# Output matmuls of a decoder layer's second attention: from bursts of four steps in shared PSUM banks to one step at a time in a bank of their own

## The chip, the cores and the metric

The kernel runs on one core of a Trainium2 chip, as one program for the whole input. The metric is the device time of one execution in microseconds; the median of three runs of the kernel before is 2312.41 us.

## What is computed

The reference is one decoder layer over x of shape (8, 512, 256), with a context of shape (8, 1024, 128): a first attention (16 heads of 16, with a convolution and a position matmul ahead of it), a layer norm, a second attention, a layer norm, and a routed feed-forward part with two more norms. The change lies in the second attention alone:

```python
q, k, v = _heads(x @ Wq + bq), _heads(x @ Wk + bk), _heads(x @ Wv + bv)
att = jnp.einsum('bhqd,bhkd->bhqk', q, k) * scale
att = jnp.where(causal[None, None], att, -jnp.inf)
y = jnp.einsum('bhqk,bhkd->bhqd', jax.nn.softmax(att, axis=-1), v)
qc = _heads(x @ Wcq + bcq)
kc, vc = _heads(cross_input @ Wck + bck), _heads(cross_input @ Wcv + bcv)
attc = jnp.einsum('bhqd,bhkd->bhqk', qc, kc) * scale
y = y + jnp.einsum('bhqk,bhkd->bhqd', jax.nn.softmax(attc, axis=-1), vc)
```

So there is a causal self attention over 512 keys and a cross attention over 1024 keys, both in fp32, for 16 heads and 8 batches.

## The kernel before, in words

Every engine has its own instruction stream, written out in Python in the order in which it runs; engines wait for each other on semaphores. The batches follow one another; the routed feed-forward part of batch b - 1 is spread through batch b.

**The steps.** The second attention of a batch is made in 48 steps (`ALL_STEPS`): 16 self steps (4 groups of 4 heads, times 4 blocks of 128 keys) and 32 cross steps (4 groups, times 8 blocks). A step s has, for each of its 4 heads g:

- a transposed score (`scoresT`, L1533): keys on the partitions, up to 512 queries in the columns, a contraction of 32 rows; in self steps it has 512, 384, 256 or 128 columns, since queries ahead of the keys are left out. ScalarE makes its exponential (`probabilities`, L651, recorded at L659) into `pT` in `work`, which holds six steps (`PT_SLOTS`); for self steps GpSimd blanks the diagonal (`causal`, L529).
- outputs (`pv`, L1558, recorded at L1570): values times probabilities, a contraction over 128 rows into 32 columns, added up over four steps (`BURST`) in one PSUM bank. In the trace each fp32 matmul stands as two instructions, so the outputs of a step are 8 rows and a burst of four steps 32.

Softmax needs a row maximum ahead of the transposed scores. For it the plain scores (`scores`, L1513 and L1517) are made seven steps ahead (`LEAD`), and VectorE reduces them (`maxima`, L1030 and L1033). Five such groups of four are made in four self steps, so that scores and maxima are through after step 36. A transpose (`max_rows`, L1530) and an addition (`put_rows`, L1055) put the maxima into a spare row of the queries. After the last burst of a group of heads its outputs are transposed (`o_transpose`, L1582), and VectorE divides and adds (`finish`, L1063 to L1069).

**The order on TensorE.** In every step a score and a transposed score alternate, head by head, on different row groups. `burst_behind` lets a whole burst of outputs follow the last pair of every fourth step, up to burst 8; from step 38 on (`SINGLES_FROM`, `SINGLES_BEHIND`) outputs are made one step at a time, two steps behind, by `pv_step`.

**The banks.** PSUM has eight banks of 512 fp32 columns. Banks 0 to 3 are VectorE's ring: scores, outputs, max rows and transposed outputs take the next of four slots in an order that `slot_uses` writes out, and `free_slot` (L1207) lets TensorE wait until VectorE has read the use four before. Banks 4 to 7 are ScalarE's ring (`exp_bank`, L377): the n-th transposed score waits for the exponential of n - 4. From step 37 on (`LATE_STEP`) there are no more scores; then ScalarE has six banks and the rest two.

```python
RING, EXP_RING = 4, 4
LATE_BANKS, LATE_EXP_BANKS = (6, 7), (4, 5, 0, 1, 2, 3)
```

**The order on VectorE.** In step s: from step 37 on first a piece of the feed-forward part of the batch before (`third_sums` at 37, `third_norm` at 39, a convolution at 40, `last_sums` at 42, `last_norm` at 44), then the step's maxima, then the read-out of a finished burst (`outputs`, L1040) where `outputs_ready` names one, in four bursts behind two transposes of the next batch's queries and keys (L761), then `put_rows` and `finish`. The read-out of burst j stands at step 4 (j + 1) up to j = 8, and at 4 (j + 1) + 1 behind that.

Of the kernel before, what the change touches and what calls it, by code (L numbers as in the profile page):

```python
# [37 lines left out]
def decoder_layer(nc, x, xT, ctxT, conv_w, pe_w, qkT, vT, outT, Wk, bk, Wq, bq, Wv, bv, Wck, bck, Wcq, bcq,  # L38
# [12 lines left out]
    NT = S // P  # L51
# [27 lines left out]
    RING, EXP_RING = 4, 4  # L79
# [17 lines left out]
    USES = ALL_SCORES + (4 + BURSTS) * HG + FFN_USES  # L97
# [18 lines left out]
    with ctx:  # L116
# [147 lines left out]
        sT_mm, pT_ready, causal_done = sem("sT_mm"), sem("pT_ready"), sem("causal_done")  # L264
        rec_step, y_done = sem("rec_step"), sem("y_done")
# [63 lines left out]
        def burst_behind(s):  # L329

            return [s // BURST - 1] if s % BURST == 0 and s > 0 else []

        def outputs_ready(s):

            j = s // BURST - 1
            return [j] if s % BURST == (0 if j < SINGLES_FROM else SINGLES_BEHIND - 1) and j >= 0 else []

        def slot_uses(ffn):
# [13 lines left out]
            for s in range(ALL_STEPS):  # L352
# [3 lines left out]
                order.extend(("pv", j) for j in outputs_ready(s))  # L356
                order.extend(("rows",) + part for part in rows_behind(s))
                order.extend(("o",) + part for part in outputs_behind(s))
            order += [("pv", ALL_STEPS // BURST - 1), ("o", CROSS, HG - 1)]
# [16 lines left out]

        def exp_bank(n):  # L377
            return bank[:, RING + n % EXP_RING if n < FIRST_LATE else LATE_EXP_BANKS[(n - FIRST_LATE) % len(LATE_EXP_BANKS)], :]

        def last_exp(at):  # L380

            return max(n for n in range(FIRST_LATE, ALL_SCORES) if LATE_EXP_BANKS[(n - FIRST_LATE) % len(LATE_EXP_BANKS)] == at)
# [173 lines left out]
        def _(act):  # L556
# [37 lines left out]
            def batch(b, prev=True, ahead=True):  # L594
# [140 lines left out]
        def _(dve):  # L735
# [206 lines left out]
            def batch(b, prev=True, ahead=2):  # L942
# [97 lines left out]
                def outputs(j):  # L1040

                    use = uses["pv", j]
                    dve.wait_ge(slot_in, base + use + 1)
                    if j < HG or j % 2 == 0:
                        nc.vector.tensor_copy(o_rows[:, SELF if j < HG else CROSS, :], slot(uses, use)).then_inc(slot_out, 1)  # L1045
                    else:
                        dve.wait_ge(slot_out, base + uses["pv", j - 1] + 1)
                        nc.vector.tensor_tensor(o_rows[:, CROSS, :], slot(uses, use), o_rows[:, CROSS, :], ALU.add).then_inc(slot_out, 1)
# [148 lines left out]
        def _(pe):  # L1197
# [112 lines left out]
            def batch(b, prev=True, ahead=True):  # L1310
# [222 lines left out]
                def scoresT(s, g):  # L1533
# [8 lines left out]
                    if n >= FIRST_LATE + len(LATE_EXP_BANKS):  # L1542
# [170 lines left out]
```

## Time and profile before

| what | value |
|---|---|
| runs | 2309.06, 2312.41, 2316.03 us; median 2312.41 us |
| span of the profiled execution | 2303.2 us, 9.2 us under the median of the runs (its own time is not listed apart from theirs) |
| TensorE, weight loads | busy 2183.0 us (95%), 991.3 us (43%) |
| VectorE | 1869.5 us (81%) |
| ScalarE | 1384.6 us (60%) |
| GpSimd | 189.0 us (8%) |
| granted TensorE clock, mean | 0.970 |

The span runs from the first to the last instruction. Times in the rows below are in us from the span's start; most are of batch 3 (the fourth), whose second attention lies at 976 to 1133. TensorE's rows overlap, since matmuls on different row or column groups run side by side and their ends are modelled, so its busy share says little of how much work it had.

### The profile page before, as it was taken

The page shows a single profiled execution, that of the slowest core. Times are in us where ns is not written, and L with a number is a line of the kernel's source. Part 1 is how long each engine was busy: PE and PEld are TensorE (multiplying, and loading weights), DVE is VectorE, ACT ScalarE, POOL GpSimd, SP SyncE. Part 2 cuts the span into 40 slices and gives each one's busy share as a digit, 9 for nine tenths or more (in the row PEclk, how much of TensorE's full clock was granted, in tenths as well). Part 3 has the DMA queues.
Part 4 walks back from the last instruction along what each step waited for, and adds up shares of the span by engine and source line. Part 5 has one row for each costly group of instructions (what it writes and reads, how often), then busy time and mean ns, then how long its engine had stood idle before and what let it go on. Part 6 is the DMA issues. An engine that isn't in the chain of part 4 may idle for free.

```text
span 2303.2 us, 37677 instructions
## 1 busy us (share of the span) xinstructions
PE 2183.0 (95%) x13138; PEld 991.3 (43%) x13138; DVE 1869.5 (81%) x5137; ACT 1384.6 (60%) x2977; POOL 189.0 (8%) x349
## 2 busy tenths in 40 slices
PE   5999999999999999999999999999999999989992
PEld 2354434543345434554335543454334543345432
DVE  6858879788888879788797887978888787978854
ACT  2834687456854579446783467745686457844560
POOL 3011001100011000110001100010001100001000
PEclk7899999999999999999999999999999999999995
DMA  3600034000520006100160002500043000510000
GB/s 110 130 10 1 1 67 81 10 1 1 113 44 10 1 19 121 27 1 1 38 119 10 2 1 58 100 10 1 1 91 57 10 1 11 105 33 1 1 10 9
DMA packets 250845, 81.69 MB, mean 35 GB/s; under 512 B 236064, under 2 KB 247328, under 8 KB 250656
## 3 DMA queue, kind: packets, MB, share of 16 engines
q1 hardware_dynamic: 250656, 79.29, 16.8%
q8 instruction: 104, 1.70, 0.3%
q14 instruction: 85, 0.70, 0.1%
HBM read 16.35 MB, written 4.19 MB: 9 GB/s over the span
## 4 chain that ended last, share of the span: by engine, by line
PE 79%; DVE 10%; ACT 7%; issue 3%; DMA 0%; SPq 0%; POOL 0%; DVEq 0%; POOLq 0%; ACTq 0%
PE bank L1517 23%; PE bank L1570 13%; PE bank L1555 7%; PE bank L1204 7%; PE bank L1513 5%; ACT work L603 4%; PE bank L1552 4%; PE bank L1470 4%; DVE work L770 4%; PE bank L1333 3%; PE bank L1320 2%; PE bank L1356 2%; PE bank L1530 2%; PE bank L1582 1%; ACT k_c L636 1%
## 5 line engine op out<-in xcount | busy, mean ns | idle before, releaser
L659 ACT ACTIVATE work<-bank 128x512 f32<-128x512 f32 (+3 forms) x1536 | 739.7, 550 | 529.8 <-PE bank L1552 264.1
L1033 DVE TENSOR_REDUCE top_half<-bank 128x1 f32<-128x512 f32 x1024 | 625.5, 682 | 21.0 <-PE bank L1517 21.0
L1517 PE MATMUL bank<-k_c,q_c 32*128 32x512 f32 x2048 | 628.6, 634 | 0.0
L1555 PE MATMUL bank<-q_c,k_c 32*128 32x512 f32 x2048 | 526.2, 633 | 0.0
L603 ACT ACTIVATE work<-work,neg 128x512 bf16<-128x512 bf16 x512 | 362.6, 715 | 30.5 <-DVE work L770 29.8
L1517 PEld LDWEIGHTS bank<-k_c,q_c 32*128 32x128 f32 x2048 | 274.6, 184 | 245.1 <-DVE top_half L1033 159.8
L770 DVE TENSOR_SCALAR_CACHE_REDUCE work<-bank 128x512 bf16<-128x512 f32 x512 | 322.4, 686 | 43.7 <-PE bank L1302 33.6
L1570 PE MATMUL bank<-work,v_flat 128*32 128x512 f32 (+3 forms) x3072 | 321.8, 544 | 5.5 <-ACT work L659 5.0
L1030 DVE CUSTOM_DVE_ANT_0 masked<-bank,mask_w 128x384 bf16<-128x384 f32 (+3 forms) x512 | 223.8, 488 | 79.5 <-PE bank L1513 74.0
L1552 PE MATMUL bank<-q_s,k_s 32*128 32x512 f32 (+3 forms) x1024 | 258.1, 471 | 0.0
L1555 PEld LDWEIGHTS bank<-q_c,k_c 32*128 32x128 f32 x2048 | 218.4, 183 | 78.4 <-ACT work L659 48.6
L1513 PE MATMUL bank<-k_s,q_s 32*128 32x384 f32 (+3 forms) x1024 | 204.5, 482 | 3.8 <-DVE top_s L1030 3.6
L1570 PEld LDWEIGHTS bank<-work,v_flat 128*32 128x32 f32 x3072 | 86.6, 109 | 236.8 <-ACT work L659 119.0
L1320 PE MATMUL bank<-k,q 32*128 32x512 bf16 x448 | 140.5, 390 | 16.4 <-DVE work L770 14.3
L1552 PEld LDWEIGHTS bank<-q_s,k_s 32*128 32x128 f32 x1024 | 141.7, 185 | 22.0 <-ACT work L659 9.1
L1513 PEld LDWEIGHTS bank<-k_s,q_s 32*128 32x128 f32 x1024 | 104.5, 187 | 81.5 <-DVE top_s L1030 41.0
L1333 PE MATMUL bank<-work,v 128*32 128x512 bf16 x512 | 133.3, 386 | 0.8 <-DMA work<-work 0.5
L529 POOL TENSOR_SCALAR_AFFINE_SELECT work<-work 128x512 f32<-128x512 f32 x128 | 81.2, 634 | 606.4 <-ACT work L659 606.4
L518 POOL TENSOR_SCALAR ln_var<-mv 128x4 f32<-128x4 f32 x32 | 8.7, 272 | 1473.8 <-DVE mv L779 1473.8
L1356 PE MATMUL bank<-k,identb 128*128 128x512 bf16 x448 | 122.0, 391 | 5.8 <-DVE work L770 3.6
L963 DVE TENSOR_SCALAR work<-work,rden 128x512 bf16<-128x512 bf16 x424 | 123.0, 350 | 4.5
L1045 DVE COPY featA<-bank 128x512 f32<-128x512 f32 x64 | 44.3, 692 | 93.6 <-PE bank L1570 93.6
(194 smaller groups left out, 2214.1 us busy)
## 6 DMA issues: line engine op xcount, KB each, us to landing
xT_pad<-xT SPq DMA_DIRECT2D x16, 256.0 KB, 3.3
ctx_sb<-ctxT SPq DMA_DIRECT2D x8, 512.0 KB, 3.4
x_res<-x SPq DMA_DIRECT2D x8, 512.0 KB, 4.8
out<-r_sb SPq DMA_DIRECT2D x8, 512.0 KB, 3.1
work<-work SPq DMA_TRANSPOSE x112, 4.4
qk_sb<-qkT SPq DMA_DIRECT2D x1, 512.0 KB, 4.7
pe_sb<-pe_w SPq DMA_DIRECT2D x1, 256.0 KB, 4.0
v_sb<-vT SPq DMA_DIRECT2D x1, 256.0 KB, 5.4
```

The costliest lines, as they stand in the source:

```text
L603: nc.scalar.activation(e1[:, h % E1_SLOTS, t, :], s1[:, h % 2, t, :], ACT.Exp, bias=neg1[:, h % 2, t:t + 1], scale=-1.0, accum_out=den1[:, ...
L659: nc.scalar.activation(pT[:, s % PT_SLOTS, g, q0:S], exp_bank(n)[:, 0:S - q0], ACT.Exp, scale=SCALE).then_inc(pT_ready, 1)
L770: nc.vector.tensor_scalar(s1[:, h % 2, t, :], bank[:, (NT * h + t) % A1_BANKS, :], -SCALE, None, ALU.mult, ALU.min, accum_out=neg1[:, h % ...
L1030: nc.vector.tensor_tensor_reduce(masked[:, g, 0:n], scores[:, 0:n], mask_w[:, S - n:S], -1.0, -MASKED, ALU.add, ALU.min, top_s[:, i % 2, u ...
L1033: nc.vector.tensor_reduce(top_half[:, i % 2, g, u // 2, u % 2:u % 2 + 1], scores, AX.X, ALU.max, negate=True).then_inc(slot_out, 1)
L1320: mm(bank[:, n % A1_BANKS, :], q_1[rows, i, P * t:P * (t + 1)], k_1[rows, i, :], start=True, stop=True, tile_position=(GW * (h % GH), 0)). ...
L1333: last = mm(bank[GW * g:GW * (g + 1), PV1_BANKS[h // 8], :], v1[:, h, j, :], p1T[:, h % E1_SLOTS, :, j, :], start=(h % 2 == 0 and j == 0), ...
L1513: mm(dst[:, 0:n], q_s[rows, i, P * u:n], k_s[rows, i, 0:n], start=True, stop=True, tile_position=(GW * g, 0)).then_inc(slot_in, 1)
L1517: mm(dst, q_c[rows, i, P * t:P * (t + 1)], k_c[rows, i, S * half:S * (half + 1)], start=True, stop=True, tile_position=(GW * g, 0)).then_i ...
L1552: mm(dst[:, 0:S - q0], k_s[rows, i, q0:q0 + P], q_s[rows, i, q0:S], start=True, stop=True, tile_position=(GW * g, 0)).then_inc(sT_mm, 1)
L1555: mm(dst, k_c[rows, i, P * u:P * (u + 1)], q_c[rows, i, :], start=True, stop=True, tile_position=(GW * g, 0)).then_inc(sT_mm, 1)
L1570: last = mm(dst[GW * g:GW * (g + 1), q0:S], v_flat[:, at:at + GW], pT[:, s % PT_SLOTS, g, q0:S], start=(s % BURST == 0), stop=(s % BURST = ...
```

## The change

- Bank 7 (`PV_BANK`) becomes the outputs' own, with two semaphores of its own: `pv_mm` is raised by each step of outputs, `pv_out` by each read-out of a burst. The first step of a burst waits for the read-out of the burst before.
- Outputs are made one step at a time in all steps, two steps behind (`PV_BEHIND`), right behind the fourth transposed score of a step. `pv` and `burst_behind` are gone.
- ScalarE's ring has three banks (4, 5, 6) up to step 36; from step 37 on it has six in another order. VectorE's ring keeps its four banks (0 to 3), and after that one (6), and outputs take no slot in it.
- ScalarE waits for a free probability slot by the step (`pv_mm`) and no longer by the burst.
- The read-out of every burst j stands at step 4 (j + 1) + 1 of VectorE's order.

```diff
-    RING, EXP_RING = 4, 4
+    RING, EXP_RING, PV_BANK = 4, 3, 7
-    SINGLES_FROM, SINGLES_BEHIND = 9, 2
+    PV_BEHIND = 2
-    LATE_BANKS, LATE_EXP_BANKS = (6, 7), (4, 5, 0, 1, 2, 3)
+    LATE_BANKS, LATE_EXP_BANKS = (6,), (5, 4, 0, 1, 2, 3)
...
         def outputs_ready(s):
-            j = s // BURST - 1
-            return [j] if s % BURST == (0 if j < SINGLES_FROM else SINGLES_BEHIND - 1) and j >= 0 else []
+            return [s // BURST - 1] if s % BURST == PV_BEHIND - 1 and s >= BURST else []
...
+        def exp_at(n):
+            return RING + n % EXP_RING if n < FIRST_LATE else LATE_EXP_BANKS[(n - FIRST_LATE) % len(LATE_EXP_BANKS)]
+        def exp_before(n):
+            return max((i for i in range(n) if exp_at(i) == exp_at(n)), default=None)
...
                     if s >= PT_SLOTS:
-                        act.wait_ge(slot_in, base + uses["pv", (s - PT_SLOTS) // BURST] + 1)
+                        act.wait_ge(pv_mm, b * ALL_STEPS + s - PT_SLOTS + 1)
...
-                    dve.wait_ge(slot_in, base + use + 1)
+                    dve.wait_ge(pv_mm, b * ALL_STEPS + BURST * (j + 1))
...
-                    if n >= FIRST_LATE + len(LATE_EXP_BANKS):
-                        pe.wait_ge(pT_ready, b * ALL_SCORES + n - len(LATE_EXP_BANKS) + 1)
-                    elif n >= FIRST_LATE + 2:
+                    if exp_before(n) is not None:
+                        pe.wait_ge(pT_ready, b * ALL_SCORES + exp_before(n) + 1)
+                    elif n >= FIRST_LATE:
                         pe.wait_ge(slot_out, base + uses["late"])
-                    elif n >= EXP_RING:
-                        pe.wait_ge(pT_ready, b * ALL_SCORES + n - EXP_RING + 1)
...
                 def pv_step(s):
-                    pv(s // BURST, range(s % BURST, s % BURST + 1))
+                    kind, i, u = part_of(s)
+                    pe.wait_ge(pT_ready, b * ALL_SCORES + GH * (s + 1))
+                    if kind == SELF:
+                        pe.wait_ge(causal_done, b * SELF_STEPS + s + 1)
+                    if s % BURST == 0 and b * PV_BURSTS + s > 0:
+                        pe.wait_ge(pv_out, b * PV_BURSTS + s // BURST)
...
+                        last = mm(bank[GW * g:GW * (g + 1), PV_BANK, q0:S], v_flat[:, at:at + GW], pT[:, s % PT_SLOTS, g, q0:S],
+                                  start=(s % BURST == 0), stop=(s % BURST == BURST - 1), tile_position=(0, GW * g))
+                    last.then_inc(pv_mm, 1)
...
                         scoresT(s, g)
-                        if g == GH - 1 and s - SINGLES_BEHIND >= BURST * SINGLES_FROM:
-                            pv_step(s - SINGLES_BEHIND)
-                    for j in burst_behind(s):
-                        if j < SINGLES_FROM:
-                            pv(j)
+                        if g == GH - 1 and s >= PV_BEHIND:
+                            pv_step(s - PV_BEHIND)
```

On TensorE, in the cross steps of the first batch, around the end of step 20, before. L1517 is a score, L1555 a transposed score, L1570 outputs; `slot_out` is raised by VectorE, `pT_ready` by ScalarE's exponentials:

```order
L1517 MATMUL bank<-k_c,q_c 128x512 [waits slot_out]
L1555 MATMUL bank<-q_c,k_c 128x512 [waits pT_ready]
L1517 MATMUL bank<-k_c,q_c 128x512 [waits slot_out]
L1555 MATMUL bank<-q_c,k_c 128x512 [waits pT_ready]
L1570 MATMUL bank<-work,v_flat 32x512 [waits slot_out,pT_ready]
L1570 MATMUL bank<-work,v_flat 32x512 x15
L1517 MATMUL bank<-k_c,q_c 128x512 [waits slot_out,pj_evac]
L1555 MATMUL bank<-q_c,k_c 128x512 [waits pT_ready]
```

The same place now (the score is at L1519, outputs at L1569):

```order
L1569 MATMUL bank<-work,v_flat 32x512 [waits pv_out,pT_ready]
L1569 MATMUL bank<-work,v_flat 32x512 x3
L1519 MATMUL bank<-k_c,q_c 128x512 [waits slot_out]
L1555 MATMUL bank<-q_c,k_c 128x512 [waits pT_ready]
L1519 MATMUL bank<-k_c,q_c 128x512 [waits slot_out]
L1555 MATMUL bank<-q_c,k_c 128x512 [waits pT_ready]
L1519 MATMUL bank<-k_c,q_c 128x512 [waits slot_out]
L1555 MATMUL bank<-q_c,k_c 128x512 [waits pT_ready]
L1519 MATMUL bank<-k_c,q_c 128x512 [waits slot_out]
L1555 MATMUL bank<-q_c,k_c 128x512 [waits pT_ready]
L1569 MATMUL bank<-work,v_flat 32x512 [waits pT_ready]
L1569 MATMUL bank<-work,v_flat 32x512 x3
```

The sixteen output matmuls that stood together behind every fourth step now stand in fours behind the four pairs of each step.

On VectorE, at the change from step 36 to step 37 of a batch that carries the feed-forward part, before (L1045 is the read-out of burst 8, L775 to L929 are `third_sums`, L1055 is `put_rows` of step 38):

```order
L1045 COPY featA<-bank 128x512 [waits slot_in]
L775 BN_STATS stats<-xs 128x6 x4
L779 BN_AGGR mv<-stats 128x2 [waits ffn_step]
L779 BN_AGGR mv<-stats 128x2 x3
L927 SCALAR_TENSOR_TENSOR xs<-xs,mv,gamma_row 128x256 [waits ln_stats2]
L927 SCALAR_TENSOR_TENSOR xs<-xs,mv,gamma_row 128x256 x3
L929 TENSOR_TENSOR r_sb<-r_sb,beta_row 128x1024
L1055 TENSOR_TENSOR q_c<-bank,q_c 128x512 [waits slot_in,ffn_step]
```

and now:

```order
L778 BN_STATS stats<-xs 128x6 x4
L782 BN_AGGR mv<-stats 128x2 [waits ffn_step]
L782 BN_AGGR mv<-stats 128x2 x3
L930 SCALAR_TENSOR_TENSOR xs<-xs,mv,gamma_row 128x256 [waits ln_stats2]
L930 SCALAR_TENSOR_TENSOR xs<-xs,mv,gamma_row 128x256 x3
L932 TENSOR_TENSOR r_sb<-r_sb,beta_row 128x1024
L1047 COPY featA<-bank 128x512 [waits pv_mm,ffn_step]
L1057 TENSOR_TENSOR q_c<-bank,q_c 128x512 [waits slot_in]
```

The read-out of burst 8 moved from ahead of the sums to behind them.

## Rows read from the trace of the kernel before

**Rows 1.** The page: the span, busy time by engine, and the chain by engine.

```profile
span 2303.2 us, 37677 instructions
...
PE 2183.0 (95%) x13138; PEld 991.3 (43%) x13138; DVE 1869.5 (81%) x5137; ACT 1384.6 (60%) x2977; POOL 189.0 (8%) x349
...
PE 79%; DVE 10%; ACT 7%; issue 3%; DMA 0%; SPq 0%; POOL 0%; DVEq 0%; POOLq 0%; ACTq 0%
```

**Rows 2.** Busy time by window of batch 3; columns in the first line.

```profile
core 0: us, PE busy (x) PEld busy (x) DVE busy (x) ACT busy (x) POOL busy (x), PEclk, DMA share, GB/s
976.00:1033.00 57.00, 57.00 (x416) 31.11 (x411) 50.21 (x132) 24.85 (x64) 10.15 (x16) 0.97 0.02 9
1033.00:1106.70 73.70, 73.65 (x552) 30.88 (x550) 63.52 (x112) 44.96 (x84) 0.00 (x0) 1.00 0.00 1
```

**Rows 3.** Timeline of TensorE, steps 24 to 27: start us, duration us, engine, line.

```profile
1060.13 0.59 PE L1555 MATMUL bank<-q_c,k_c 32*128 32x512 f32 x1
1060.65 3.64 PE L1570 MATMUL bank<-work,v_flat 128*32 128x512 f32 x32
...
1064.23 0.69 PE L1555 MATMUL bank<-q_c,k_c 32*128 32x512 f32 x1
...
1064.76 0.59 PE L1555 MATMUL bank<-q_c,k_c 32*128 32x512 f32 x1
...
1065.19 0.59 PE L1517 MATMUL bank<-k_c,q_c 32*128 32x512 f32 x1
...
1066.13 0.69 PE L1555 MATMUL bank<-q_c,k_c 32*128 32x512 f32 x1
...
1071.37 0.66 PE L1582 MATMUL bank<-ident,featA 128*128 128x128 f32 x4
1071.96 0.69 PE L1517 MATMUL bank<-k_c,q_c 32*128 32x512 f32 x1
...
1074.48 0.64 PE L1570 MATMUL bank<-work,v_flat 128*32 128x512 f32 x4
```

**Rows 4.** Timeline of ScalarE, the first exponential behind that burst.

```profile
1065.48 0.60 ACT L659 ACTIVATE work<-bank 128x512 f32<-128x512 f32 x1 [4.09 <-PE bank L1555]
```

**Rows 5.** Timeline of VectorE in the same stretch.

```profile
1064.36 0.69 DVE L1048 TENSOR_TENSOR featA<-bank,featA 128x512 f32<-128x512 f32 x1 [1.22 <-PE bank L1570]
1065.38 7.27 DVE L1033 TENSOR_REDUCE top_half<-bank 128x1 f32<-128x512 f32 x12 [0.33 <-PE bank L1517]
```

**Rows 6.** Timeline of TensorE, steps 37 to 42.

```profile
1105.59 3.48 PE L1555 MATMUL bank<-q_c,k_c 32*128 32x512 f32 x16
1108.99 1.07 PE L1570 MATMUL bank<-work,v_flat 128*32 128x512 f32 x8
1109.99 0.66 PE L1530 MATMUL bank<-ident,top_c 128*128 128x128 f32 x4
...
1119.46 1.07 PE L1570 MATMUL bank<-work,v_flat 128*32 128x512 f32 x8 [1.00 <-ACT work L659]
```

**Rows 7.** Timeline of VectorE, step 37.

```profile
1106.32 1.39 DVE L775 BATCH_NORM_STATS2 stats<-xs 128x6 f32<-128x256 f32 x4
...
1109.86 1.22 DVE L929 TENSOR_TENSOR r_sb<-r_sb,beta_row 128x1024 f32<-128x1024 f32 x1
```

**Rows 8.** Self steps: windows (two batches), then timelines of TensorE and ScalarE.

```profile
702.30:727.00 24.70, 24.70 (x190) 14.90 (x187) 21.99 (x82) 12.15 (x32) 5.08 (x8) 1.00 0.06 21
976.00:1002.30 26.30, 26.30 (x196) 15.63 (x193) 22.45 (x83) 12.15 (x32) 5.08 (x8) 0.94 0.05 19
1002.30:1017.40 15.10, 15.10 (x118) 7.58 (x112) 13.71 (x24) 6.36 (x16) 2.54 (x4) 0.99 0.00 1
1017.40:1033.00 15.60, 15.60 (x116) 7.89 (x112) 14.05 (x26) 6.34 (x16) 2.54 (x4) 1.00 0.00 1
...
1005.68 0.58 PE L1552 MATMUL bank<-q_s,k_s 32*128 32x384 f32 x1
...
1006.93 1.25 ACT L659 ACTIVATE work<-bank 128x384 f32<-128x384 f32 x3 [2.32 <-PE bank L1552]
```

More of the change, by code:

```diff
@@ L355, in slot_uses @@
                 take_maxima(maxima_before(s), maxima_before(s + 1))
-                order.extend(("pv", j) for j in outputs_ready(s))
                 order.extend(("rows",) + part for part in rows_behind(s))
                 order.extend(("o",) + part for part in outputs_behind(s))
-            order += [("pv", ALL_STEPS // BURST - 1), ("o", CROSS, HG - 1)]
+            order += [("o", CROSS, HG - 1)]
             assert len(order) == (USES if ffn else USES - FFN_USES)
@@ L375, in decoder_layer @@
         LAST_BURST = ALL_STEPS // BURST - 1
+        def exp_at(n):
+            return RING + n % EXP_RING if n < FIRST_LATE else LATE_EXP_BANKS[(n - FIRST_LATE) % len(LATE_EXP_BANKS)]
         def exp_bank(n):
-            return bank[:, RING + n % EXP_RING if n < FIRST_LATE else LATE_EXP_BANKS[(n - FIRST_LATE) % len(LATE_EXP_BANKS)], :]
+            return bank[:, exp_at(n), :]
+        def exp_before(n):
+            return max((i for i in range(n) if exp_at(i) == exp_at(n)), default=None)
         def last_exp(at):
-            return max(n for n in range(FIRST_LATE, ALL_SCORES) if LATE_EXP_BANKS[(n - FIRST_LATE) % len(LATE_EXP_BANKS)] == at)
+            return max(n for n in range(FIRST_LATE, ALL_SCORES) if exp_at(n) == at)
         def transposed(b, h):
@@ L1556, in scoresT @@
                            tile_position=(GW * g, 0)).then_inc(sT_mm, 1)
-                def pv(j, steps=range(BURST)):
-                    first, last_step = BURST * j + steps[0], BURST * j + steps[-1]
-                    pe.wait_ge(pT_ready, b * ALL_SCORES + GH * (last_step + 1))
-                    if j < HG:
-                        pe.wait_ge(causal_done, b * SELF_STEPS + NT * (j + 1))
-                    dst = free_slot(b, base, uses, uses["pv", j]) if steps[0] == 0 else slot(uses, uses["pv", j])
-                    for s in range(first, last_step + 1):
-                        kind, i, u = part_of(s)
-                        q0, tile = (P * u, u) if kind == SELF else (0, NT + u)
-                        for g in range(GH):
-                            at = tile * H * (HD + 1) + (GH * i + g) * (HD + 1)
-                            last = mm(dst[GW * g:GW * (g + 1), q0:S], v_flat[:, at:at + GW], pT[:, s % PT_SLOTS, g, q0:S],
-                                      start=(s % BURST == 0), stop=(s % BURST == BURST - 1), tile_position=(0, GW * g))
-                    if last_step % BURST == BURST - 1:
-                        last.then_inc(slot_in, 1)
@@ L1575, in pv_step @@
-                def pv_step(s):
-                    pv(s // BURST, range(s % BURST, s % BURST + 1))
+                def pv_step(s):
+                    kind, i, u = part_of(s)
[4 more added lines that the diff above has]
+                        pe.wait_ge(pv_out, b * PV_BURSTS + s // BURST)
+                    q0, tile = (P * u, u) if kind == SELF else (0, NT + u)
+                    for g in range(GH):
+                        at = tile * H * (HD + 1) + (GH * i + g) * (HD + 1)
+                        last = mm(bank[GW * g:GW * (g + 1), PV_BANK, q0:S], v_flat[:, at:at + GW], pT[:, s % PT_SLOTS, g, q0:S],
+                                  start=(s % BURST == 0), stop=(s % BURST == BURST - 1), tile_position=(0, GW * g))
+                    last.then_inc(pv_mm, 1)
```

15 lines of the change are left out of this document (7 added, 8 removed).

## The prediction

> **What bounds the kernel now.** First the busy shares [rows 1]: TensorE reads 95%, VectorE 81%, and the chain that ended last lies on TensorE for 79%. That does not say that TensorE works at its limit: its rows overlap, and a matmul that follows late still leaves its engine "busy". So next the same batch cut into stages [rows 2]: in the second attention of one batch 57.0 us go to the sixteen self steps, 73.7 us to the cross steps while maxima are still being made (steps 16 to 36). VectorE is busy 63.5 of the 73.7 us, ScalarE 45.0.
>
> Then the timeline from one output burst to the next [rows 3 to 5]. A burst of four steps occupies TensorE from 1060.65 to 1064.22, 3.57 us. Behind it the banks are free: pairs of score and transposed-score matmuls start at once, and the next pairs follow at 1065.19. From 1066.13 on pairs come at the pace of VectorE's maxima, twelve in 7.27 us, 0.60 each. In the burst VectorE runs dry (two idle times, 1.22 and 0.33 us). So four steps cost 1074.48 - 1060.65 = 13.83 us: 3.57 for the burst, 1.91 until the first maximum has been read, then pairs at VectorE's pace with a transpose among them. VectorE sets the pace between bursts, TensorE in them. What the change means to recover is VectorE's idle time there; the question is what it pays.
>
> **The part that decides: three banks and a burst in every step.** Two durations are needed.
>
> The round trip of a ScalarE bank: the first transposed score behind a burst starts at 1064.23 [rows 3]; ScalarE, idle by then, starts on it at 1065.48 and takes 0.60 us [rows 4]. That is 1.85 us, and TensorE's next start behind a release comes about 0.05 later (VectorE's first maximum ends at 1065.38 + 0.69 = 1066.07 [rows 5], the pair that waits for its bank starts at 1066.13). So a bank can be written again 1.91 us after its last write began.
>
> The tail of a matmul before outputs: a transposed score runs as two halves 0.53 us apart (1064.23 and 1064.76), and the outputs start 0.52 us behind the second half (1060.13 to 1060.65) [rows 3]. Outputs read all row groups, so nothing overlaps there: 1.05 us from a transposed score's start to the outputs.
>
> The outputs of a single step: 1108.99 to 1109.99, 1.00 us [rows 6], against 3.57 / 4 = 0.89 for a quarter of a burst.
>
> Now the new order of a cross step on TensorE: pair 0, pair 1, pair 2, pair 3, outputs of the step before last. With three banks the fourth transposed score of a step needs the bank of the first one *of the same step*. The first cannot start before the outputs of the step before are issued, since the queue is in order. So every step holds one whole round trip: 1.91 (first to fourth transposed score) + 1.05 (fourth to outputs) + 1.00 (outputs) = **3.96 us a step**. With four banks the fourth would have started at 0.96 behind the first, as at 1065.19 [rows 3], and the step would be about 2.9 to 3.0. Nothing else is longer than 3.96: four maxima are 2.4 us and VectorE's other work some 0.5 a step; four exponentials are at most 4 x 0.60 = 2.4. VectorE will idle some 1 us in each step where it now idles 1.55 in four.
>
> Steps 16 to 36: 21 x 3.96 = 83.2, plus five groups of transposes at 0.59 (1071.37 to 1071.96 [rows 3]) = 3.0, less 1.1 since the outputs at steps 16 and 17 are of short self steps: 85.0 us. Now 73.7 [rows 2]. **+11.3 us a batch.**
>
> On the drain: the last half before outputs is followed after 0.52 us, where halves of pairs follow each other after 0.43 (1064.76 to 1065.19), and a single step costs 1.00 against 0.89 [rows 3, 6]. The Trainium skill (TensorEngine Tiling (Array Packing), Key Properties) says that changing the tiling mode drains the TensorE; this change goes between 32-row and 32-column tiles four times as often. Its cost by these rows, 4 x 0.11 + 3 x 0.09 = 0.7 us in four steps, is already in the 3.96; by that rule alone, with no ring in the way, the 21 steps would lose 3.7 us a batch and the kernel 30 us, if VectorE's idle time gave nothing back.
>
> **Self steps.** The transposed scores have 512, 384, 256 and 128 columns. Step u = 0: 1.91 + 1.05 + 0.55 (outputs of 256 columns) = 3.5. u = 1: ScalarE's first 384-column exponential starts 1.25 us behind its matmul (1005.68 to 1006.93) and takes about 0.5 [rows 8], so 1.8 + 0.8 + 0.33 = 2.9. u = 2: shorter again, but with outputs of 512 columns, about 3.3. u = 3 has eight scores and goes by VectorE's 0.60 pace [rows 5]: 3.7 + 1.05 + 0.78 = 5.5. With two groups of transposes 16.4 us for four steps, against 15.1 and 15.6 in two such groups [rows 8]: +1. The first eight steps, where outputs now start at step 2 and scores are short, I put at 29 against 24.7 to 26.3 [rows 8]: +3. Together **+5 a batch**. Bounds: 0 if VectorE's backlog covers the round trips (u = 3 leaves TensorE ahead), +8 if it covers none and the causal select adds to them.
>
> **Late steps** (37 to 47). Six banks for ScalarE as before, in another order: nothing. One step of outputs (step 35) moves in here from the last burst; it runs while TensorE would wait in any case, for this: the read-out of burst 8 now stands in VectorE's queue behind the third layer norm's sums (before, it stood ahead of them), and outputs of step 36 wait for it. The sums run 1106.32 to 1111.08, 4.8 us [rows 7]. They will start where the last maximum ends, about 0.3 us before step 37's first matmul: 4.5, plus 0.69 for the copy = 5.2 us; TensorE is there after some 3.3 and waits 1.9. Now these outputs start 3.4 us behind step 37's first matmul (1105.59 to 1108.99 [rows 6]), so +1.8. Behind that, the read-out of burst 9 ends late now and makes TensorE wait 1.00 us at 1119.46 [rows 6]; I let 0.4 of the delay be swallowed there. Net **+1.4 a batch**, in the seven batches that carry these sums; bounds 0 and +3.
>
> Edits with no price: ScalarE's wait for a free probability slot goes by step instead of by burst (slots are six steps deep, outputs two steps behind, ScalarE busy 45.0 of 73.7 us [rows 2]), VectorE's four score banks are no longer lent to outputs (it idles in any case, so this gives nothing once TensorE's round trip decides), the read-out of each burst must be done before the next burst's first step; it has a step of almost 4 us for 0.69, plus 1.4 of query transposes in four bursts.
>
> **Sum.** 8 x (11.3 + 5) + 7 x 1.4 = 140 us. The profiled span is 2303.2 [rows 1], 9.2 under the median of 2312.4; the difference is carried over. 2312.4 + 140 = **2452 us**. Own range of this case: 8 x 11.3 alone gives 2403; 8 x (11.3 + 8 + 3), with 0.1 us more in each of 21 steps, gives 2508.
>
> **Rivals.**
> *The ring does not bind (faster).* If the fourth transposed score were not held, for instance because ScalarE returned the first bank within about 1.0 us, four steps would cost what TensorE itself needs: 4 x 2.85 + 0.6 = 12.0 us, and VectorE's 9.6 + 0.7 + halves of its other work about the same. For 21 steps that is 64 to 65 against 73.7, some 9 a batch, with 0.5 from the self steps: -76 us, 2236. The point from which it decides: a step costs 3.37 us now ((73.7 - 3.0) / 21), so a round trip under 3.37 - 2.05 = 1.3 us would win. For it: VectorE's idle time in bursts is real, 1.22 + 0.33 us [rows 5]. Against it: 1.25 us of matmul and 0.60 of exponential stand in the rows [rows 3, 4]. 0.07.
> *The two cancel.* The round trip costs only in cross steps and half of it is caught up, since the steps could fall into a rhythm where the first bank is released earlier: within 10 us of now. 0.03: the queue's order leaves no such rhythm that I can find.
> *The clock falls too (slower still).* TensorE now stands still in each step. In the self stage it already stands waiting, and the stretch 976 to 1002.3 has a granted clock of 0.94, where the same steps of the batch before had 1.00 and took 24.7 instead of 26.3 [rows 8]. The same loss of 7% over the 85 us of these steps adds 48: 2500. The Trainium skill (TensorE: Matmul & The Clock Gate, A second HAM failure mode) tells of a kernel that cycles through PSUM banks and falls to half clock and back. The cross stage here shows 1.00 [rows 2]. 0.07.
> *The forecast*: 0.83.
>
> **Numbers.** 0.3% of the time, 7 us, is about what a measurement can tell from no change. Faster 0.07, same 0.03, slower 0.90. Range 2400 to 2515: it takes in the forecast's bounds and the clock case.
>
> **What would show it.** In the profile after: cross steps at 3.9 to 4.0 us each; in each one transposed score that starts about 1.9 us behind the first one, TensorE's weight loads waiting for ScalarE's exponentials (L659's line) and no longer for VectorE; VectorE idle over 1 us a step before its first maximum, waiting for TensorE; output matmuls in groups of eight with 1.00 us each; a wait of 1 to 2 us of the outputs in step 38 for VectorE's copy. I am wrong if cross steps come at 3.0 us with VectorE's maxima without a gap, or if the fourth transposed score starts within 1.2 us of the first.

## The result, and the profile after

The changed kernel takes **2469.5 us** (median of 4 runs, 2467.87 to 2473.88), the kernel before 2311.55 on the same chip (4 runs): 1.069 times as long, 95% interval 1.0673 to 1.0710. The forecast was 2452 us, with a range of 2400 to 2515 and a chance of 0.90 for slower.

The page of the changed kernel, the lines that answer to [rows 1]:

```profile
span 2472.1 us, 37773 instructions
...
PE 2333.0 (94%) x13138; PEld 958.9 (39%) x13138; DVE 1885.1 (76%) x5137; ACT 1394.3 (56%) x2977; POOL 189.7 (8%) x349
...
PE 78%; DVE 10%; ACT 7%; issue 3%; DMA 1%; SPq 0%; POOL 0%; DVEq 0%; POOLq 0%; ACTq 0%
```

The same work on VectorE and ScalarE (1885 and 1394 us, before 1870 and 1385), and 150 us more of "busy" TensorE with as many matmuls. The page alone would be read as "TensorE bound, as before", which is wrong. The windows of batch 3, to be laid beside [rows 2] and [rows 8]: steps 0 to 3, 4 to 7, 8 to 11, 12 to 15, then 16 to 36, then 37 to 46, each from the start of its first step's first exponential (which starts 1.25 us behind the first transposed score in the cross steps):

```profile
core 0: us, PE busy (x) PEld busy (x) DVE busy (x) ACT busy (x) POOL busy (x), PEclk, DMA share, GB/s
1040.40:1053.40 13.00, 13.00 (x100) 7.16 (x94) 10.17 (x43) 6.24 (x16) 2.55 (x4) 1.00 0.08 33
1053.40:1069.60 16.20, 15.49 (x115) 7.55 (x114) 12.29 (x41) 6.35 (x16) 2.55 (x4) 1.00 0.01 2
1069.60:1086.10 16.50, 16.48 (x115) 7.67 (x112) 14.17 (x25) 6.35 (x16) 2.55 (x4) 1.00 0.00 1
1086.10:1102.70 16.60, 16.58 (x115) 7.69 (x113) 14.45 (x26) 6.35 (x16) 2.55 (x4) 1.00 0.00 1
1102.70:1187.60 84.90, 84.90 (x528) 26.80 (x526) 64.37 (x112) 45.61 (x84) 0.00 (x0) 1.00 0.00 1
1187.60:1213.20 25.60, 23.00 (x168) 6.85 (x168) 16.75 (x40) 20.54 (x40) 2.80 (x4) 1.00 0.13 42
```

The cross steps go from 73.7 to 84.9 us at a granted clock of 1.00, with TensorE "busy" all the time. The table sums such stretches over the eight batches, in every kernel of this study (each stretch runs from the start of the first exponential of its first step to that of the step behind its last; "rest" is the span less the other three):

| kernel (profiled run) | steps 0-15 | 16-36 | 37-46 | rest | span |
|---|---|---|---|---|---|
| before | 449.2 | 587.9 | 188.7 | 1077.3 | 2303.2 |
| after | 508.0 | 679.7 | 203.7 | 1080.7 | 2472.1 |
| x1 before, three ScalarE banks | 484.3 | 634.3 | 188.8 | 1074.7 | 2382.1 |
| x2 after, three VectorE, four ScalarE | 636.3 | 687.3 | 207.7 | 1168.3 | 2699.6 |
| x3 after, outputs by two steps | 479.9 | 617.1 | 215.8 | 1080.9 | 2393.7 |
| x4 after, head 0's exponential halved | 501.0 | 643.5 | 212.4 | 1071.4 | 2428.2 |
| x5 after, heads 1 and 2 halved | 514.5 | 680.0 | 203.9 | 1074.1 | 2472.5 |
| x6 after, earlier read-out | 520.9 | 680.1 | 192.9 | 1072.7 | 2466.6 |
| x7 after, outputs by two heads | 544.4 | 731.0 | 207.3 | 1077.7 | 2560.3 |
| x8 after, outputs by three heads | 534.2 | 697.5 | 210.4 | 1082.8 | 2524.9 |
| x9 after, no fourth transposed score | 510.3 | 536.7 | 214.7 | 1072.1 | 2333.8 |
| x10 after, head 0's exponential an eighth | 506.0 | 617.8 | 210.7 | 1082.3 | 2416.9 |

Of the 168.9 us between the two spans 91.8 lie in the cross steps, 58.8 in the self steps, 15.0 in the late ones and 3.4 elsewhere.

One cross step of the changed kernel, on TensorE (start us, duration us; the answer to [rows 3]):

```profile
1140.16 1.07 PE L1569 MATMUL bank<-work,v_flat 128*32 128x512 f32 x8
...
1141.16 0.69 PE L1555 MATMUL bank<-q_c,k_c 32*128 32x512 f32 x1
...
1142.56 0.60 PE L1519 MATMUL bank<-k_c,q_c 32*128 32x512 f32 x2
1143.07 1.12 PE L1555 MATMUL bank<-q_c,k_c 32*128 32x512 f32 x2
1144.12 1.07 PE L1569 MATMUL bank<-work,v_flat 128*32 128x512 f32 x8
```

Outputs follow outputs after 3.96 us. The first transposed score starts at 1141.16, the fourth at 1143.07, 1.91 us later and alone: all four scores of the step are out by then. ScalarE and VectorE in the same step (answer to [rows 4, 5]):

```profile
1142.42 1.57 ACT L662 ACTIVATE work<-bank 128x512 f32<-128x512 f32 x3 [1.55 <-PE bank L1555]
1144.23 0.60 ACT L662 ACTIVATE work<-bank 128x512 f32<-128x512 f32 x1 [0.23 <-PE bank L1555]
```

```profile
1138.36 2.48 DVE L1036 TENSOR_REDUCE top_half<-bank 128x1 f32<-128x512 f32 x4 [1.47 <-PE bank L1519]
1140.76 0.70 DVE L764 STREAM_TRANSPOSE q<-qk_nat 128x512 bf16<-128x512 bf16 x1
```

ScalarE idles 1.55 us in each step, VectorE up to 1.47 in some. Where TensorE waits is seen in its weight loads only. Groups of steps 16 to 36 in the same batch, first of the changed kernel, then of the one before (idle time before them, and what ended it, at the end of the line):

```profile
L1036 DVE TENSOR_REDUCE top_half<-bank 128x1 f32<-128x512 f32 x84 | 52.1, 682 | 15.3 <-PE bank L1519 15.3
L1555 PEld LDWEIGHTS bank<-q_c,k_c 32*128 32x128 f32 x170 | 20.0, 183 | 24.2 <-ACT work L662 16.6 <-issue 7.6
L1519 PEld LDWEIGHTS bank<-k_c,q_c 32*128 32x128 f32 x160 | 14.5, 184 | 13.1 <-DVE top_half L1036 9.8 <-issue 2.5 <-DVE y_sb L1067 0.2
```

```profile
L1033 DVE TENSOR_REDUCE top_half<-bank 128x1 f32<-128x512 f32 x84 | 51.2, 681 | 1.7 <-PE bank L1517 1.7
L1555 PEld LDWEIGHTS bank<-q_c,k_c 32*128 32x128 f32 x175 | 22.2, 183 | 2.7 <-issue 2.0 <-DVE featA L1045 0.6
L1517 PEld LDWEIGHTS bank<-k_c,q_c 32*128 32x128 f32 x163 | 21.6, 183 | 21.8 <-DVE top_half L1033 15.4 <-issue 4.4 <-DVE y_sb L1065 0.4
```

Before, loads for transposed scores never waited for ScalarE and loads for scores waited for VectorE's maxima: VectorE set the pace. Now transposed scores wait 16.6 us for ScalarE's exponentials, and the maxima wait 15.3 us for TensorE instead of 1.7. The loads for scores still wait 9.8 us for VectorE's maxima, so VectorE has not gone from the picture altogether.

### The profile page after: what moved, and what is told of

Its sections match the earlier page's. It is cut to its first block, busy times and chain, and to the rows that moved or that the text cites. A ratio compares the mean times of both kernels' runs of the same rounds, so it can differ in the third digit from the quotient of the medians.

```text
span 2472.1 us, 37773 instructions
## 1 busy us (share of the span) xinstructions
PE 2333.0 (94%) x13138; PEld 958.9 (39%) x13138; DVE 1885.1 (76%) x5137; ACT 1394.3 (56%) x2977; POOL 189.7 (8%) x349
## 4 chain that ended last, share of the span: by engine, by line
PE 78%; DVE 10%; ACT 7%; issue 3%; DMA 1%; SPq 0%; POOL 0%; DVEq 0%; POOLq 0%; ACTq 0%
PE bank L1555 16%; PE bank L1519 13%; PE bank L1569 13%; PE bank L1206 6%; PE bank L1552 6%; PE bank L1515 5%; ACT work L606 4%; PE bank L1472 4%; DVE work L773 3%; PE bank L1335 3%; PE bank L1322 2%; PE bank L1358 2%; PE bank L1532 2%; PE bank L1577 1%; ACT work L662 1%
## 5 line engine op out<-in xcount | busy, mean ns | idle before, releaser
L662 ACT ACTIVATE work<-bank 128x512 f32<-128x512 f32 (+3 forms) x1536 | 749.1, 545 | 686.0 <-PE bank L1555 372.9
L1036 DVE TENSOR_REDUCE top_half<-bank 128x1 f32<-128x512 f32 x1024 | 634.1, 682 | 155.7 <-PE bank L1519 155.7
L1555 PE MATMUL bank<-q_c,k_c 32*128 32x512 f32 x2048 | 621.4, 634 | 0.0
L1519 PE MATMUL bank<-k_c,q_c 32*128 32x512 f32 x2048 | 531.1, 623 | 0.0
L1569 PE MATMUL bank<-work,v_flat 128*32 128x512 f32 (+3 forms) x3072 | 370.9, 557 | 16.7 <-DVE featA L1047 8.4
L1555 PEld LDWEIGHTS bank<-q_c,k_c 32*128 32x128 f32 x2048 | 201.9, 184 | 252.8 <-ACT work L662 173.0
L1552 PE MATMUL bank<-q_s,k_s 32*128 32x512 f32 (+3 forms) x1024 | 280.0, 472 | 6.0 <-ACT work L662 3.6
L1519 PEld LDWEIGHTS bank<-k_c,q_c 32*128 32x128 f32 x2048 | 203.5, 185 | 148.8 <-DVE top_half L1036 92.4
L1569 PEld LDWEIGHTS bank<-work,v_flat 128*32 128x32 f32 x3072 | 61.8, 108 | 287.6 <-ACT work L662 264.8
L1322 PE MATMUL bank<-k,q 32*128 32x512 bf16 x448 | 140.5, 390 | 16.2 <-DVE work L773 14.3
L1515 PEld LDWEIGHTS bank<-k_s,q_s 32*128 32x128 f32 x1024 | 97.6, 186 | 77.1 <-issue 35.1
L606 ACT ACTIVATION_READ_ACCUMULATOR work<-work,neg 128x1 bf16 x512 | 100.8, 197 | 0.0
```

Of the source, the lines that this page charges most:

```text
L606: nc.scalar.activation(e1[:, h % E1_SLOTS, t, :], s1[:, h % 2, t, :], ACT.Exp, bias=neg1[:, h % 2, t:t + 1], scale=-1.0, accum_out=den1[:, ...
L662: nc.scalar.activation(pT[:, s % PT_SLOTS, g, q0:S], exp_bank(n)[:, 0:S - q0], ACT.Exp, scale=SCALE).then_inc(pT_ready, 1)
L1036: nc.vector.tensor_reduce(top_half[:, i % 2, g, u // 2, u % 2:u % 2 + 1], scores, AX.X, ALU.max, negate=True).then_inc(slot_out, 1)
L1322: mm(bank[:, n % A1_BANKS, :], q_1[rows, i, P * t:P * (t + 1)], k_1[rows, i, :], start=True, stop=True, tile_position=(GW * (h % GH), 0)). ...
L1515: mm(dst[:, 0:n], q_s[rows, i, P * u:n], k_s[rows, i, 0:n], start=True, stop=True, tile_position=(GW * g, 0)).then_inc(slot_in, 1)
L1519: mm(dst, q_c[rows, i, P * t:P * (t + 1)], k_c[rows, i, S * half:S * (half + 1)], start=True, stop=True, tile_position=(GW * g, 0)).then_i ...
```

## Experiments

Ten kernels ran. The theory is that of the prediction: with three banks each step holds a whole round trip of one bank.

### Three banks alone (x1)

The kernel before, with its bursts and with outputs in VectorE's ring, but three banks for ScalarE (its waits rewritten to name the last user of a bank, as in the change).

```diff
-    RING, EXP_RING = 4, 4
+    RING, EXP_RING = 4, 3
```

> The kernel before, with its bursts of four steps kept and ScalarE's ring cut from four banks to three (bank 7 lies idle up to step 36). Theory A (one round trip of 1.91 us is put between outputs in every step): three banks alone set a pace of 1.91 / 3 = 0.64 us for a pair where VectorE's is 0.60; sixteen pairs behind a burst hold five round trips, 9.55 + 1.05 + 3.57 = 14.2 us without transposes against some 13.4 now. +4 us a batch in steps 16 to 36, +32 in all and a little more from the self steps: about 2345 us. Rival B (three banks are the whole loss, wherever the outputs stand): near 2470. Rival C (the loss is the drain at eight changes of the tile shape instead of two, the ring has no part): 2312.

Measured: 2382.85 us, 1.033 times before (1.0311 to 1.0354): more than twice the loss I had put down. The cost of three banks is not confined to steps with single outputs. TensorE behind a burst of this kernel:

```profile
1109.54 0.69 PE L1559 MATMUL bank<-q_c,k_c 32*128 32x512 f32 x1
...
1111.44 0.69 PE L1559 MATMUL bank<-q_c,k_c 32*128 32x512 f32 x1
```

The fourth transposed score again starts 1.90 us behind the first. In batch 3 a step behind a burst takes 2.36 us where before it took 1.92, the step with the burst 6.53 instead of 6.00 to 6.39, one with transposes 3.55 instead of 3.44; together 1.1 us a burst. Cross steps +46.3 us, self steps +35.1 (a part of these is clock: in batch 3 steps 8 to 11 took 18.7 us at a granted clock of 0.83), late steps +0.1 (there ScalarE has six banks in either kernel). So about half of the cross steps' loss comes with the bank alone; the other half needs the outputs in every step.

### The ring that gives the bank (x2)

```diff
-    RING, EXP_RING, PV_BANK = 4, 3, 7
+    RING, EXP_RING, PV_BANK = 3, 4, 7
```

> The changed kernel with the rings swapped: VectorE's has three banks, ScalarE's four, outputs keep bank 7. Theory A: the fourth score of a step now waits for the first maximum of the same step, 1.15 + 0.68 + 0.05 = 1.88 us, behind it 1.05 and 1.00 as before: 3.93 us a cross step, and self steps with eight scores go at 0.63 instead of 0.60 us: 2465 to 2500. Rival D (what costs is ScalarE's short ring as such, with VectorE's there is room since its engine idles): 3.0 to 3.4 us a cross step, 2300 to 2380.

Measured: 2700.67 us, 1.171 times before (1.1676 to 1.1741), 200 us above the expected range. In the cross steps as expected: 687.3 us against 679.7, most steps again exactly 3.96. The round trip of one of VectorE's banks (matmul and 0.69 us of maximum) is no shorter. What I had left out is that VectorE's ring also serves the self steps, where the last step of each four has eight scores, and the stage ahead of them: 128.3 us more than the changed kernel in steps 0 to 15 and 87.6 in the rest. Two rows of its windows, steps 4 to 7 and 16 to 36 of batch 3:

```profile
1151.90:1177.50 25.60, 24.41 (x113) 11.18 (x110) 12.82 (x41) 6.35 (x16) 2.54 (x4) 0.57 0.00 1
1215.40:1301.40 86.00, 85.25 (x528) 25.54 (x528) 66.25 (x112) 45.61 (x84) 0.00 (x0) 1.00 0.00 1
```

In the first the granted clock is 0.57, near the lower of its two levels (1.2 of 2.4 GHz), over work that takes 16.2 us at 1.00 in the changed kernel. The loss here is waits and clock together; this run doesn't separate them.

### Which part of the round trip counts (x4, x5, x10)

Exponentials of steps 16 to 36 on fewer columns, of the head whose bank the fourth transposed score takes (x4: half, x10: 64 of 512) and of the two between (x5: half). Each leaves that part of the exponentials out.

```diff
-                        nc.scalar.activation(pT[:, s % PT_SLOTS, g, q0:S], exp_bank(n)[:, 0:S - q0], ACT.Exp,
+                        cols = (S - q0) // 2 if g == 0 and SELF_STEPS <= s < LATE_STEP else S - q0
+                        nc.scalar.activation(pT[:, s % PT_SLOTS, g, q0:q0 + cols], exp_bank(n)[:, 0:cols], ACT.Exp,
```

(x5: `g in (1, 2)`; x10: `cols = 64`.)

> The changed kernel; in steps 16 to 36 the exponential of head 0 alone is made over 256 of its 512 columns, the rest is left out. Theory A: this exponential is the one in the round trip that holds the fourth transposed score. It falls from 0.60 to 0.38 us, so each of 21 steps falls by 0.22 us to 3.74: -4.6 us a batch, -37 in all, 2433. Rival C (drains) and any theory that has TensorE or VectorE set the step: 2470, no change.

> The changed kernel; in steps 16 to 36 the exponentials of heads 1 and 2 are made over 256 of their 512 columns, the rest is left out: twice as much work of ScalarE is taken away as where head 0 alone is cut. Theory A: neither is in the round trip that decides, 2470, no change, steps at 3.96 us. Rival F (ScalarE's amount of work sets the step): twice the gain of the run with head 0, 0.4 us a step, 2395.

> The changed kernel with the exponential of the first head in steps 16 to 36 on 64 of its 512 columns (the other columns keep old values: work left out). The halved one took 0.21 us off each step (84.91 to 80.43 us for 21 steps, 0.60 to 0.39 us an exponential). Theory (the first head's bank is on the path that sets the step, all of it): the step falls by what this exponential gets shorter, to about 0.2 us, so by 0.37 to 0.42 us from 3.96; steps 16 to 36 76 to 77.5 us, the whole 2400 to 2415. Rival (only part of the wait is the bank's, something else ends just behind it): no more than the 0.21 us of the half, 2435 or above.

Measured: x4 2438.42 us, ratio 1.0566 (1.0542 to 1.0589); x5 2471.09, 1.0715 (1.0699 to 1.0731); x10 2416.38, 1.0490 (1.0460 to 1.0521). The 21 steps of a batch take 80.43, 84.91 and 77.07 us, against 84.91. Less work for ScalarE on two heads changes nothing; on the one head whose bank comes back, half of the columns is worth 0.21 us a step and seven eighths 0.37: all that the instruction gets shorter (0.60 us to 0.39 and to 0.22), and no floor is reached. This is the path that sets a cross step.

The whole gained less than the cross steps (x4 is 5 us above its forecast, x10 1 above its range), since the late steps grew by 8.7 and 7.0 us. In x4 the outputs of step 36 wait 2.23 us for the read-out instead of 2.02, and from the end of that wait the granted clock is at its lower level for 3.4 us (so in six of the seven batches that have it), so that they take 1.94 us instead of 1.06. In x10 the wait is 2.38 us, and the same happens in part of the batches. A row and a window of x4:

```profile
1172.26 1.94 PE L1570 MATMUL bank<-work,v_flat 128*32 128x512 f32 x8 [2.23 <-DVE featA L1048]
...
1172.20:1175.20 3.00, 2.94 (x16) 0.98 (x16) 0.00 (x0) 0.00 (x0) 0.00 (x0) 0.50 0.00 0
```

### Fewer, larger groups (x3)

```diff
                         if g == GH - 1 and s >= PV_BEHIND:
-                            pv_step(s - PV_BEHIND)
+                            if s > LATE_STEP:
+                                pv_step(s - PV_BEHIND)
+                            elif s % 2:
+                                pv_step(s - PV_BEHIND - 1)
+                                pv_step(s - PV_BEHIND)
```

> The changed kernel, but outputs of two steps together behind every second step up to step 37 (three and two steps behind); banks and rings as in the change. Theory A: eight transposed scores stand between outputs, with three banks that holds two round trips: 2 x 1.91 + 1.05 + 1.9 = 6.8 us for two steps, 3.4 a step instead of 3.96: -10.5 us a batch from steps 16 to 36, -2 to -4 from the self steps, about 2350 to 2385 us. Rival C (drains): half of the changes of tile shape, worth 0.1 us a step: about 2450. Rival E (a bank of its own and steady outputs are what costs, by VectorE's later read-out): 2465 to 2475.

Measured: 2390.08 us, 1.0366 (1.0347 to 1.0384), 80 us less than the changed kernel and 5 above the expected range. Cross steps alternate between 2.36 us (without outputs) and 4.82 (with two steps' outputs), 3.59 on average, not the 3.4 expected. I had let two steps end with the second return of the first bank, 3.82 us in. But the eighth transposed score also needs a bank, that of the fifth: in steps 24 and 25 the first transposed score starts at 1100.82, the fifth's exponential ends at 1105.03, and the eighth starts at 1105.08, 4.26 us in. So the cross steps gave back 62.6 us instead of 84. The late steps grew by 12.1 us; in some 7 of these it is only that the outputs of step 34 (0.88 us a batch) are now made there.

### Groups by heads (x7, x8)

If outputs came behind every second or third pair, no whole round trip would lie between two groups. Core of the edit (`groups` is `{n: 2 for n in range(1, 16, 2)}` in x7, `{2: 3, 5: 3, 8: 3, 11: 3, 13: 2, 15: 2}` in x8; `pv_heads` makes the output matmuls of the heads from one number to another):

```diff
-                        if g == GH - 1 and s >= PV_BEHIND:
-                            pv_step(s - PV_BEHIND)
+                        done = GH * (s - PV_BEHIND) + g + 1
+                        ...
+                        elif s >= PV_BEHIND and (done - 1) % (GH * BURST) in groups:
+                            pv_heads(done - groups[(done - 1) % (GH * BURST)], done)
```

> The changed kernel with its output matmuls in groups of two heads, behind the second and the fourth pair of a step, instead of four heads behind the fourth: as many matmuls, twice as many changes between transposed scores and outputs. Theory (what a step costs is the round trips of ScalarE's three banks that lie whole between two groups of outputs): with two transposed scores between groups there is none; the ring then only sets its own pace. By hand: scores at 0 and 0, outputs 1.05 to 1.6, third pair 1.6, fourth at 1.9 when the first bank comes free, outputs 2.95 to 3.5: 3.5 us a cross step instead of 3.96, steps 16 to 36 75 to 78 us instead of 84.9, the whole 2385 to 2410. Rival (the changes of tiling are what costs, 1.05 us of tail and a dearer group each): one more group a step, 4.3 us or more, 2525 and up.

> The changed kernel with output matmuls in groups of three, three, three, three, two and two heads in four steps (never more than three transposed scores between two groups, 1.5 groups a step). Theory: no whole round trip lies between groups, 1.05 + 0.75 us of outputs and about 0.8 for the pairs in three pairs: 3.4 to 3.5 us a cross step, steps 16 to 36 74 to 77 us, the whole 2375 to 2400, at or a little below the groups of two. Rival (cost per change of tiling): 3.96 plus half a group, 4.1 us a step, 2460 to 2500.

Measured: x7 2561.53 us, 1.1096 (1.1073 to 1.1119); x8 2506.74, 1.0854 (1.0834 to 1.0874). Both theory's numbers are missed by over 100 us, and the rival's figures are met or nearly so. (x8's profiled run in the table is 18 us over its median; 34 us in the self steps of its batch 5 ran at the lower clock.) TensorE in x7, half a step:

```profile
1176.15 1.05 PE L1570 MATMUL bank<-work,v_flat 128*32 128x512 f32 x4
...
1177.14 0.69 PE L1555 MATMUL bank<-q_c,k_c 32*128 32x512 f32 x1
...
1177.67 0.59 PE L1519 MATMUL bank<-k_c,q_c 32*128 32x512 f32 x1
...
1178.21 1.05 PE L1570 MATMUL bank<-work,v_flat 128*32 128x512 f32 x4
```

No transposed score waits here: those of both pairs start together at 1177.14 (over the 21 steps the loads for transposed scores wait 1.0 us for ScalarE, in x8 1.3, in the changed kernel 16.6). But the outputs of two heads take from 1176.15 to 1177.14, 0.99 us, and those of four heads in the changed kernel 1.00. In the trace the first halves of four heads start within 0.02 us of each other and the second halves 0.45 us later; two heads take the same two rounds. So does a group for three heads in x8 (1180.30 to 1181.29, 0.99 us). Half a group costs as much as a whole one, the step is 2 x 2.05 = 4.11 us, and VectorE and ScalarE idle for a good part of it. My by-hand sum took 0.55 for half a group; with 1.0 it gives these 4.1. The two runs therefore say nothing against the round trip, but they don't say anything for it either, and the rival had to be tested in another way.

### No fourth transposed score (x9)

The rival that x7 left standing: the group of outputs in every step, with its two changes of tiling, is what costs. Here all of that stays, and only the transposed score that needs a bank of its own step is left out (the third one counts for two).

```diff
+        def three(n):
+            return GH * SELF_STEPS <= n < GH * LATE_STEP
+
         def exp_at(n):
+            if three(n):
+                return RING + min(n % GH, 2)
...
+                    if three(n) and g == 3:
+                        return
```

> The changed kernel without the transposed score of the fourth head in steps 16 to 36 (left out there; ScalarE's exponential for that head reads the third head's bank instead, so that ScalarE's work, VectorE's work, the outputs and every change of tiling stay). A transposed score runs beside scores in other row groups, so TensorE itself saves little by it; but no transposed score then needs the bank of one of the same step. Theory (the round trip of the three banks is what a step waits for): a step falls from 3.96 to what TensorE and VectorE need without it, 2.9 to 3.1 us; steps 16 to 36 64 to 68 us instead of 84.9, the whole 2300 to 2340. Rival (the group of outputs in each step and its two changes of tiling are what costs, and x7's slow result is the sign of it): the step keeps at least 3.6 us, the whole stays above 2410.

Measured: 2339.79 us, 1.0167 (1.0132 to 1.0202). Steps 16 to 36 of batch 3, then the outputs of two steps in a row within them:

```profile
1052.80:1120.10 67.30, 65.35 (x480) 24.34 (x476) 62.58 (x109) 43.36 (x84) 0.00 (x0) 1.00 0.00 1
```

```profile
1092.21 1.06 PE L1576 MATMUL bank<-work,v_flat 128*32 128x512 f32 x8
...
1095.13 1.06 PE L1576 MATMUL bank<-work,v_flat 128*32 128x512 f32 x8
```

67.3 us instead of 84.9, 73.5 before. Nearly half of the 21 steps come at 2.92 us, with the outputs and their changes of tiling in each; most of the others hold transposes or more of VectorE's work and take 3.1 to 4.2. VectorE is busy 62.6 of the 67.3 us. So of the 3.96 us about 1.0 is the wait for the bank (and whatever the left out matmul itself would take beside the scores), and by this run the single outputs, left to themselves, would have won at most 6 us a batch. That is work left out and no version to keep; the rival falls, since it asked for at least 3.6 us a step, and the average is 3.2.

### The read-out behind the third sums (x6)

```diff
-                sf.mark(nc.vector.tensor_tensor(r_sb[:], r_sb[:], over_tiles(beta_row), ALU.add))
+                if between:
+                    between()
+                sf.mark(nc.vector.tensor_tensor(r_sb[:], r_sb[:], over_tiles(beta_row), ALU.add))
```

(`between` is the read-out of burst 8.)

> The changed kernel; in step 37 VectorE reads burst 8 out ahead of the last addition of the third layer norm's sums (1.2 us earlier) instead of behind it. Theory A: TensorE's wait for this read-out in step 38 falls from about 1.9 to 0.6 us; a part comes back as a longer wait for the read-out of burst 9. Steps 37 to 47: from 25.65 to between 24.3 and 25.0 us, 5 to 9 us in all, 2460 to 2465. Rival: VectorE's queue as a whole ends the late steps, then nothing changes.

Measured: 2468.19 us, 1.0695 (1.0678 to 1.0713), the changed kernel's time. The outputs of step 36 with the wait in front, in the changed kernel (its first row is the start of step 37) and here:

```profile
1186.44 1.14 PE L1555 MATMUL bank<-q_c,k_c 32*128 32x512 f32 x8
...
1191.94 1.06 PE L1569 MATMUL bank<-work,v_flat 128*32 128x512 f32 x8 [2.02 <-DVE featA L1047]
```

```profile
1188.22 1.06 PE L1572 MATMUL bank<-work,v_flat 128*32 128x512 f32 x8 [0.75 <-DVE featA L1049]
```

The wait falls from 2.02 to 0.75 us, a batch's late steps from 25.65 to 24.45, in sum 10.8 us. The gain hardly shows in the whole (the span is 5.5 us shorter, the median 1.3, where 5 to 9 were expected): in this profiled run the column "rest" is 8.0 us lower, but steps 0 to 15 took 12.9 us more. Steps 4 to 7 of batch 4, for one, took 19.1 us, with this row, where the changed kernel's above took 16.2 at 1.00:

```profile
1342.90:1362.00 19.10, 18.39 (x114) 8.34 (x113) 12.43 (x41) 6.34 (x16) 2.54 (x4) 0.83 0.00 0
```

The changed kernel has such stretches too, fewer of them. Which batches are hit differs from kernel to kernel; what decides it stays open.

No run beats the kernel before. With these rings, outputs in every step need nine banks, four for either ring and one, and there are eight; x2 and the changed kernel are the two ways to be one short in a ring.

## Why the prediction was right

**The cross step (3.96 us): right.** 1140.16 to 1144.12 is 3.96, made of 1.00, 1.91 and 1.05 as forecast. +11.3 us a batch was put down, +11.5 came (679.7 - 587.9 = 91.8 in eight). x4, x5 and x10 show that the first head's bank sets it, x9 that without it most steps without other work take what TensorE and VectorE need, 2.9.

**Self steps (+5): too small, the first eight.** The 16.4 us for each four of steps 8 to 15 came as 16.55. The 29 us of steps 0 to 7 came as 12.95 + 16.23 = 29.18 wherever the clock held. What failed is the other side of the difference: I took it between 24.7 and 26.3, and 26.3 is of a batch with a clock of 0.94; at 1.00 the kernel before takes 24.70. So +4.5 and not +3 in these, +1.1 and +0.9 in the two later fours; the sum is 6.5 a batch at a clock of 1.00. With stretches at a lower clock it is 7.3 (58.8 in eight batches), 19 us over the forecast in the whole.

**Late steps (+1.4): right mechanism, a little small.** The wait for VectorE's copy stands there with 2.02 us, forecast 1.9. The stretch grows by 15.0 us in all, forecast 7 x 1.4 = 9.8. The delay was put 0.3 too low: the outputs of step 36 start 5.50 us behind step 37's first matmul (1186.44 to 1191.94), forecast 5.2, before 3.4. The 0.4 were swallowed behind it as forecast in batches 2 to 4 (step 42 of batch 3 takes 2.99 us, before 3.41), which makes +1.65 in each. In batches 1 and 5 the clock fell to its lower level behind this wait and they grew by 3.0 and 2.6; the last two batches had no later wait to swallow anything and grew by 2.4 and 2.1. x6 moves the read-out and takes 10.8 back.

**Edits at no price.** x1 lacks them, and has the late steps of before; what is left behind the terms named, 3.4 us in the rest of the span, is no more than the spread among the kernels of the table (x2 aside). I see no cost of the probability slots; no run changes them alone.

**The sum.** 140 us were forecast, 168.9 lie between the spans, 158 between the medians: the span of before lies 8.4 us under its median, that of the changed kernel 2.6 above its own. So the change was mis-sized by 18 us in the medians, and the forecast time, counted from 2312.4, is 17.5 us too low.

**Rivals.** *The ring does not bind* falls at its point: the bank comes back after 1.9 us, not 1.3. Its price was a little too good: it said 64 to 65 us for the 21 steps, and with the wait taken away (x9) they are 67.3. *The two cancel* falls with it. *The clock falls too* put the loss in the cross steps; these have 1.00 and 84.9 us in seven of eight batches, 0.99 and 85.3 in one. A part of it came true in the self steps, some 7 us, and some 2 in the late ones. The Trainium skill (TensorE: Matmul & The Clock Gate, A second HAM failure mode), which tells of falls to half clock in a kernel that cycles through PSUM banks, describes x2's 0.57 better than the changed kernel.

**The drain.** Rows show a start 0.52 us behind the last half of the other kind, against 0.43 to 0.45 behind one of the same kind, here as before. x9's steps hold two such changes and many of them still take 2.92 us. The rule of the Trainium skill (TensorEngine Tiling (Array Packing), Key Properties), that a change of mode drains the TensorE, agrees in sign. Its price here is some 0.1 us a change by these starts; the first halves behind a change also stand 0.53 us ahead of the second ones instead of 0.43, but so they do behind a mere wait (the two rows at 1143.07 take 0.53 + 0.59 = 1.12 us), so that is not the drain's alone.

**What was to show it.** The steps, the fourth transposed score 1.91 us behind, loads for transposed scores waiting for ScalarE, groups of eight with 1.00 us and the wait in step 38 are all there. That the loads would no longer wait for VectorE came only in part: 9.8 us of such waits are left before scores, of 15.4. VectorE's idle time before its first maximum was to be over 1 us a step; it is 1.47 in some and 0.73 on average (15.3 / 21), since its other work falls into the gap.

## To carry over

When a buffer is moved from a ring to a new use, write down the queue's order between two points that block it, count the tiles, and see whether the last needs the buffer of the first: if so, a whole round trip (write, read, release) lies in every such stretch, and no engine's busy share shows it. Look at what the weight loads wait for, not at how busy TensorE reads. And compare the two sides of a difference at the same clock.

## What the hardware showed that I had not expected

- A group of output matmuls for two heads takes 0.99 us (x7), for three heads 0.99 (x8), for four heads 1.00: a group that leaves some of the four column groups empty saves nothing here. I had put 0.55 on it.
- Taking the fourth bank from ScalarE costs 76 us even where outputs come in bursts (x1), since a step behind a burst takes 2.36 us with three banks for ScalarE, and 1.92 with four.
- The granted clock falls to 0.57 in a self stretch of x2 in which TensorE reads busy for 24.4 of 25.6 us. In x4 it falls to the lower level at the end of a single wait of 2.23 us, in six of seven batches; in the changed kernel the same wait is 2.02 us, and the clock falls in two batches of seven.
